# 64-row matmuls on separate row halves of the array for the fifth pass of gate and up

## Chip, cores and metric

One core of one Trainium2 chip. The metric is the device time of one execution in microseconds (us), the median of several runs. Profiles are of one execution, taken by the hardware profiler.

## What is computed

A small vision tower on 16 images of 96 x 96: patches with shifted copies are normalised and projected to 192 features, a class token is put in front (37 positions per image, 592 tokens), one attention layer with 12 heads follows, then a feed-forward layer of experts. The change lies in the last:

```python
probs = softmax(x @ router_w)                    # 8 experts, the best two are kept
g = silu(einsum('bsd,edh->bseh', x, w_gate));  u = einsum('bsd,edh->bseh', x, w_up)
routed = sum_e dense_g[e] * ((g * u) @ w_down[e])               # 8 experts of 192
shared = silu(x @ ws_gate) * (x @ ws_up) @ ws_down              # 768 hidden
alpha = sigmoid(x @ sg_w + sg_b)
h = h + alpha * shared + (1 - alpha) * routed
```

## The kernel before, in words

Everything is transposed for TensorE: features on partitions, tokens in columns (592, padded to 640, two halves of 296 columns). Products are made with near single precision from float16 operands: each operand is split into a high and a low part, and three products (high x high, low weights x high tokens, high weights x low tokens) are added up in PSUM. The 192 features are 128 + 64, so:
- `XAh`, `XAl`: high and low part of token features 0 to 127; `Ah`, `Al` the same of the weights.
- `XB`: the high part of features 128 to 191, twice, in rows 0 to 63 and 64 to 127. `Bw`: the high part of those weights in rows 0 to 63, their low part in rows 64 to 127. One matmul of 128 rows makes two of the products.
- `YC`: the low part of features 128 to 191 in rows 0 to 63, zeros in rows 64 to 127. It lies in the storage of the tile `wring`, and the profile shows it by that name. The memset at L936 clears rows 64 to 127 once the ring's weights have been used.

So each product over the features takes five passes: Ah x XAh, Al x XAh, Bw x XB, Ah x XAl, Bw x YC. In the fifth, half of the array's rows multiply by zeros.

Feed-forward stage on TensorE: the hidden units are 18 blocks `f` of 128 (6 shared, 12 of experts). `gu(i)` with i = 2f + half makes gate (m = 0) and up (m = 1) of one block and one half of the tokens, ten matmuls of 296 columns into two PSUM banks (L580). It waits until product i - 2 has been made (`v_hf`). `down(f)` (L608) has 15 matmuls of 192 columns. The order is gu(2f), gu(2f+1), down(f-2). Between gu's first and second five matmuls of i = 0 stands `router()` (L556, L558): for each of five token tiles the five passes with 9 columns (`YC` and `WC` with 97 rows) and a sixth for the bias. `gates(k)` (L590) transposes the gates in the middle of steps 6 and 7.

Behind each gu(i): ScalarE makes silu of the gate (L817); for experts GpSimd (L863) or, where a block belongs to two experts, VectorE (L1258, two instructions of 64 rows) multiplies by the gate values; VectorE multiplies by up (L1269, `product`); ScalarE rounds to float16 (L824, `ah`), GpSimd takes the rest (L872, `al`). Between these, by fixed places in the code, VectorE does the steps of choosing experts (L1209 to L1245), and ScalarE and VectorE prepare the weights of the next pieces (L719, L972, `ffn_high` and `ffn_low`). After step 15 VectorE adds the shared part into `acc` (L1292). Tokens' high parts come from ScalarE (L736, L737), low parts from VectorE (L1061, `low_parts`).

Of the kernel before, what the change touches and what calls it, by code (L numbers as in the profile page):

```python
# [24 lines left out]
P = 128  # L25
IMAGES, POSITIONS, D = 16, 37, 192
N = IMAGES * POSITIONS
HALF = N // 2
# [17 lines left out]
QC, KC, VC, OC, RC = 0, 384, 768, 960, 1152  # L46
AW = RC + 9
CROWS = 97
# [7 lines left out]
SX, SW, SPIX, SPW, SK, SQ, SP_, SV, SCTX, SH = 64.0, 64.0, 16.0, 256.0, 16.0, 4.0, 256.0, 16.0, 16.0, 16.0  # L56
# [4 lines left out]
FRONT = 3 * P  # L61
# [20 lines left out]
def vit_kernel(nc, x_inner, x_ring, w_inner, w_ring, gb, consts, j_rev, ind, tok_b, cls, tab,  # L82
               aw_a, aw_b, aw_c, f_a, f_b, f_d, gate_rows, out):
    with ExitStack() as ctx:
        def sb(name, shape, dt=F32):
            return ctx.enter_context(nc.sbuf_tensor(name, shape, dt))

        def sem(name):
            return ctx.enter_context(nc.semaphore(name))

        PS = ctx.enter_context(nc.psum_tensor("PS", [P, 8, 512], F32))
# [48 lines left out]
        XAh, XAl, XB = (sb(n, [P, NPAD], F16) for n in ("XAh", "XAl", "XB"))  # L140
        XC = sb("XC", [CROWS, NPAD], F16)
        YC = wring[:, :, :].rearrange("p r d -> p (r d)")[:, 0:NPAD // 2].bitcast(F16)
# [3 lines left out]
        WAh, WAl, WB = (sb(n, [P, AW], F16) for n in ("WAh", "WAl", "WB"))  # L146
        WC = sb("WC", [CROWS, AW], F16)
# [25 lines left out]
        def stages(p):  # L173
            r = (stage, stage, xhl)[p]
            ab = r[:, 0:4 * PC].rearrange("p (k g c) -> p k g c", k=2, g=2)
            return ab[:, 0], ab[:, 1], r[:, 4 * PC:4 * PC + PT_ * D].rearrange("p (f d) -> p f d", f=PT_)

        def split(p):
            r = (piece0, slab, xsq)[p]
            up = r[:, 0:3 * PC].bitcast(F16).rearrange("p (k g c) -> p k g c", k=3, g=2)  # L180
            dn = r[:, 3 * PC:3 * PC + PT_ * D].bitcast(F16).rearrange("p (k f d) -> p k f d", k=2, f=PT_)
            return up[:, 0], up[:, 1], up[:, 2], dn[:, 0], dn[:, 1]
# [25 lines left out]
                   a_first a_xh a_xsq a_s0 a_ring a_bw a_sqr a_cs a_aw a_wh a_sqrt a_hi a_kh a_q1 a_vh a_exp a_pth a_chi a_e a_dup a_sig a_gt  # L208
                   a_fw a_silu a_ah
                   v_one v_ind v_pad v_aw0 v_jm v_jr v_xl v_fold v_wl v_awl v_mk v_stat v_h v_hn v_lo  v_kk v_q2 v_vm v_xr v_sg v_max v_sub  # L210
                   v_rows v_cn v_rd v_lg v_gate v_gx v_fw v_hf v_acc v_fin v_al v_bn
                   g_one g_sg g_al""".split()
        S = {n: sem(n) for n in names}

# [4 lines left out]

            return [XAh[:, cols], XAh[:, cols], XB[:, cols], XAl[:, cols], XC[:, cols]]  # L220

        def yparts(cols, rows=P):

            return [XAh[:, cols], XAh[:, cols], XB[:, cols], XAl[:, cols], YC[0:rows, cols]]

        def wparts(c0, c1):

            return [WAh[:, c0:c1], WAl[:, c0:c1], WB[:, c0:c1], WAh[:, c0:c1], WC[:, c0:c1]]

        def pair_cols(C, p, rows):  # L230

# [62 lines left out]
        def _(pe):  # L294
            mm = nc.tensor.matmul
# [61 lines left out]
            for t in range(TILES):  # L357
                last = mm(PS[:, 1, t:t + 1], sqrows[:, t * P:(t + 1) * P], one[:, :], start=(t == 0), stop=True,
                          skip_group_check=True)
# [4 lines left out]
            for t in range(TILES):  # L364
                tok = slice(t * P, (t + 1) * P)
                mm(PS[:, (6, 6, 7, 7, 2)[t], D * (t % 2):D * (t % 2) + D], inds[:, tok], biasrow[:, :],
                   start=(t % 2 == 0), stop=True, skip_group_check=True).then_inc(S["p_bias"], 1)
# [23 lines left out]
            def tokens_ready(n, half, k):  # L391

                if k in (0, 2):
                    pe.wait_ge(S["a_hi"], 4 * n + 2 * half + (1 if k == 0 else 2))
                if k in (3, 4):
                    pe.wait_ge(S["v_lo"], 4 * n + 2 * half + (1 if k == 3 else 2))
# [4 lines left out]
            for f in range(12):  # L401
                q, g, half = kq_product(f)
                if f == 3:
                    transposes(0, (1, 2, 0), (3, 4))
                c0 = (QC if q else KC) + g * P
                if f >= 4:
                    q4, g4, half4 = kq_product(f - 4)
                    pe.wait_ge(S["v_q2" if q4 else "v_kk"], GROUPS * half4 + g4 + 1)
                cols = slice(half * HALF, (half + 1) * HALF)
                for i, (w, x) in enumerate(zip(wparts(c0, c0 + P), xparts(cols))):  # L410
                    if f in (0, 6):
                        tokens_ready(0, half, i)
                    last = mm(PS[:, 3 + f % 4, 0:HALF], w, x, start=(i == 0), stop=(i == 4))  # L413
                last.then_inc(S["p_q" if q else "p_k"], 1)
# [132 lines left out]

            def router():

                pe.wait_ge(S["v_rows"], 1)  # L550
                pe.wait_ge(S["a_hi"], 8)
                pe.wait_ge(S["v_lo"], 8)
                for t in range(TILES):
                    tok = slice(t * P, (t + 1) * P)
                    for k, (x, w) in enumerate(zip(yparts(tok, CROWS), wparts(RC, RC + 9))):
                        mm(PS[:, 7, 9 * t:9 * t + 9], x, w, start=(t == 0 and k == 0), stop=False,  # L556
                           skip_group_check=True)
                    last = mm(PS[:, 7, 9 * t:9 * t + 9], XO[:, :], WC[:, RC:RC + 9], start=False, stop=True,  # L558
                              skip_group_check=True)
                last.then_inc(S["p_r"], 1)  # L560

            def gu(i):

                f, half = divmod(i, 2)
                if i % (2 * PT_) == 0:
                    pe.wait_ge(S["a_fw"], 6 * (f // PT_) + 6)
                    pe.wait_ge(S["v_fw"], 6 * (f // PT_) + 6)
                if i >= 2:
                    pe.wait_ge(S["v_hf"], i - 1)
                cols = slice(half * HALF, (half + 1) * HALF)  # L570
                Ah, Al, Bw, _, _ = split(f // PT_)
                fc = slice(f % PT_ * P, (f % PT_ + 1) * P)
                for m in range(2):
                    if i == 0 and m == 1:
                        router()
                    w5 = (Ah[:, m, fc], Al[:, m, fc], Bw[:, m, fc], Ah[:, m, fc], Bw[:, m, fc])
                    for k, (w, x) in enumerate(zip(w5, yparts(cols))):
                        if i < 2 and m == 0:
                            tokens_ready(1, i, k)
                        last = mm(PS[:, 3 + 2 * (i % 2) + m, 0:HALF], w, x, start=(k == 0), stop=(k == 4))  # L580
                last.then_inc(S["p_gu"], 1)

            def gates(k):
# [30 lines left out]
            for f in range(FT + 2):  # L614
                for half in range(2):
                    if f < FT:
                        gu(2 * f + half)
                    if 0 <= 2 * f + half - GATE_STEP < 2:
                        gates(2 * f + half - GATE_STEP)
                if f >= 2:  # L620
                    down(f - 2)
# [261 lines left out]
        def _(dve):  # L883
            V = nc.vector
# [48 lines left out]

            dve.wait_ge(S["v_wl"], 4)
            dve.wait_ge(S["p_bw"], 1)
            V.memset(YC[64:P, :], 0.0).then_inc(S["v_rows"], 1)  # L936
            V.memset(CA[:, N:NPAD], 0.0)
            V.memset(CC[:, N:NPAD], 0.0)

# [25 lines left out]
            def ffn_low(p, q):  # L965

                Ah, Al, Bw, Dh, Dl = split(p)
                k, m = divmod(q, 2)
                W, hi, st, r0 = (Al, Bw, Dl)[k], (Ah, Bw, Dh)[k], stages(p)[k], (0, 64, 0)[k]
                part = slice(3 * m, 3 * m + 3) if k == 2 else slice(m, m + 1)  # L970
                dve.wait_ge(S["a_fw"], 6 * p + q + 1)
                V.scalar_tensor_tensor(out=W[r0:P, part], in0=st[r0:P, part], scalar=SW, in1=hi[r0:P, part],  # L972
                                       op0=ALU.mult, op1=ALU.subtract).then_inc(S["v_fw"], 1)

            for k in range(3):
# [76 lines left out]
                                    ALU.subtract, ALU.mult).then_inc(S["v_hn"], 1)  # L1052

            def low_parts(n, banks, part):
                a, b = ((PS[:, banks[0], 0:FRONT], PS[0:64, banks[1], 0:FRONT]) if part == 0 else
                        (PS[:, banks[2], 0:2 * P], PS[0:64, banks[2], 2 * P:4 * P]))
                cols = slice(0, FRONT) if part == 0 else slice(FRONT, NPAD)
                for k, (dst, src, hi) in enumerate(((XAl[:, cols], a, XAh[:, cols]),
                                                     ((XC, YC)[n][0:64, cols], b, XB[0:64, cols]))):
                    dve.wait_ge(S["a_hi"], 4 * n + (k + 1 if part == 0 else 4))  # L1060
                    V.scalar_tensor_tensor(out=dst, in0=src, scalar=SX, in1=hi, op0=ALU.mult,  # L1061
                                           op1=ALU.subtract).then_inc(S["v_lo"], 1)
# [209 lines left out]
            for i in range(2 * FT):  # L1272
# [15 lines left out]
                if i == 2 * ST + 3:  # L1288

                    dve.wait_ge(S["p_dn"], ST)  # L1290
                    for t in range(TILES):
                        V.scalar_tensor_tensor(out=acc[:, t, :], in0=PS[:, t // 2, D * (t % 2):D * (t % 2) + D],  # L1292
                                               scalar=small[:, 38, t:t + 1], in1=h2[:, t, :], op0=ALU.mult,
# [5 lines left out]
            for t in range(TILES):  # L1299
                dve.wait_ge(S["p_end"], t // 2 + 1)  # L1300
                V.scalar_tensor_tensor(out=fin[:, t, 0:D], in0=PS[:, t // 2, D * (t % 2):D * (t % 2) + D],
                                       scalar=1.0 / (SH * SW), in1=acc[:, t, :], op0=ALU.mult,
# [112 lines left out]
```

## Time and profile before

| | |
|---|---|
| median of 3 runs | 173.03 us (172.47 to 173.92) |
| the profiled execution | 173.96 us, its span 172.2 us |
| TensorE busy | 147.6 us, 86% of the span, 1714 matmuls |
| VectorE busy | 121.1 us, 70% |
| ScalarE busy | 90.7 us, 53% |
| GpSimd busy | 41.3 us, 24% |

The span is the time from the first to the last instruction of the program in the profile; the execution's own time has about 1.8 us more around it. PE is TensorE's matmuls, PEld its weight loads, DVE VectorE, ACT ScalarE, POOL GpSimd. A matmul's start is recorded, its end is modelled; matmuls overlap, so a row's time is more than its share of the engine, and the distance between starts tells the rate. Times of rows are us from the start of the span.

### The profile page before, as it was taken

How to read it: one execution, taken by the hardware profiler on the slowest of the kernel's cores; microseconds unless marked ns; L12 is line 12 of the kernel's file. 1: busy time of each engine (PE TensorE's matmuls, PEld its weight loads, DVE VectorE, ACT ScalarE, POOL GpSimd, SP SyncE). 2: the span in 40 equal slices, each digit the busy share in tenths (PEclk: the TensorE clock that was granted, in tenths of full speed). 3: DMA queues.
4: the chain of work that ended last, by engine and by line, in shares of the span. 5: the costliest groups of instructions: out<-in, count | busy, mean ns of one | idle time of the engine just before them, and what ended most of it. 6: DMA issues, size and time to landing. Idle time of an engine off the chain costs nothing.

```text
span 172.2 us, 4275 instructions
## 1 busy us (share of the span) xinstructions
PE 147.6 (86%) x1714; PEld 114.3 (66%) x1714; DVE 121.1 (70%) x297; ACT 90.7 (53%) x198; POOL 41.3 (24%) x55
## 2 busy tenths in 40 slices
PE   0439999949799988939999689999899999999992
PEld 0218777923467977838964468788777778888782
DVE  6299953999899997992378299976695663542753
ACT  0588879630577725533237768756645434343340
POOL 0000010000000000000000035336947858578430
PEclk9999999999999999995699999999999999999999
DMA  5999999000000000007990000048300000000003
GB/s 148 380 368 373 337 229 353 7 0 0 0 0 4 4 4 4 4 0 213 386 371 41 4 0 0 4 117 319 134 4 0 0 0 4 4 0 4 0 0 106
DMA packets 7391, 16.89 MB, mean 98 GB/s; under 512 B 800, under 2 KB 3612, under 8 KB 7372
## 3 DMA queue, kind: packets, MB, share of 16 engines
q1 hardware_dynamic: 7012, 16.29, 27.8%
q10 hardware_dynamic: 360, 0.34, 0.7%
q8 instruction: 13, 0.21, 0.5%
q14 instruction: 6, 0.05, 0.1%
HBM read 16.15 MB, written 0.47 MB: 97 GB/s over the span
## 4 chain that ended last, share of the span: by engine, by line
PE 53%; DVE 28%; ACT 6%; issue 4%; DMA 4%; POOL 2%; SPq 0%; DVEq 0%; POOLq 0%
PE PS L580 20%; PE PS L608 11%; DMA xs<-in_x_inner_dram 4%; PE PS L413 3%; DVE xsq L1128 3%; DVE mx L1124 2%; PE PS L322 2%; DVE piece L972 2%; PE PS L475 2%; PE PS L425 2%; DVE hn L1051 2%; PE PS L343 2%; PE PS L345 2%; PE PS L346 2%; PE PS L309 2%
## 5 line engine op out<-in xcount | busy, mean ns | idle before, releaser
L872 POOL TENSOR_TENSOR kq<-vhl,kq 128x296 f16<-128x296 f32 x35 | 28.7, 820 | 95.1 <-ACT kq L824 95.1
L1269 DVE SCALAR_TENSOR_TENSOR vhl<-PS,vhl 128x296 f32<-128x296 f32 x36 | 16.7, 465 | 21.0 <-POOL vhl L863 12.1
L817 ACT ACTIVATE vhl<-PS 128x296 f32<-128x296 f32 x36 | 14.9, 416 | 26.2 <-PE PS L580 26.2
L824 ACT ACTIVATE kq<-vhl 128x296 f16<-128x296 f32 x36 | 16.1, 446 | 5.7 <-DVE vhl L1269 5.7
L863 POOL TENSOR_TENSOR vhl<-vhl,xs 128x296 f32<-128x296 f32 x14 | 12.6, 902 | 5.5 <-issue 4.8
L1258 DVE TENSOR_TENSOR vhl<-vhl,xs 64x296 f32<-64x296 f32 (+1 forms) x18 | 10.2, 566 | 2.8 <-ACT vhl L817 2.6
L580 PE MATMUL PS<-XAh,piece 128*128 128x296 f16 x48 | 10.0, 289 | 2.0 <-DVE vhl L1269 1.9
L372 PE MATMUL PS<-WAh 128*128 128x512 f16 x41 | 9.5, 379 | 2.5 <-DVE small L1020 2.2
L580 PE MATMUL PS<-XAh,slab 128*128 128x296 f16 x48 | 10.0, 290 | 0.9 <-DVE vhl L1269 0.9
L343 PE MATMUL PS<-whl,xhl 128*128 128x193 f16 (+1 forms) x40 | 10.5, 262 | 0.0
L345 PE MATMUL PS<-whl,xhl 128*128 128x193 f16 (+1 forms) x40 | 10.5, 262 | 0.0
L923 DVE SCALAR_TENSOR_TENSOR we<-slab,gbs,we 128x192 f32<-128x192 f32 x24 | 8.1, 409 | 3.2 <-ACT we L664 3.2
L346 PE MATMUL PS<-whl,xhl 128*128 128x192 f16 (+1 forms) x40 | 10.4, 259 | 0.0
L309 PE MATMUL PS<-slab,gbs 128*32 128x192 f32 x60 | 4.5, 396 | 6.5 <-DMA slab<-in_w_inner_dram 6.5
L580 PE MATMUL PS<-XAh,xsq 128*128 128x296 f16 x48 | 10.0, 290 | 0.0
L372 PEld LDWEIGHTS PS<-WAh 128*128 128x128 f16 x41 | 3.7, 97 | 7.8 <-issue 2.5
L608 PE MATMUL PS<-slab,kq 128*128 128x192 f16 x90 | 8.4, 246 | 0.3 <-DVE t L1292 0.3
L608 PE MATMUL PS<-piece,kq 128*128 128x192 f16 x90 | 8.4, 246 | 0.0
L608 PE MATMUL PS<-xsq,kq 128*128 128x192 f16 x90 | 8.2, 246 | 0.1
L608 PEld LDWEIGHTS PS<-slab,kq 128*128 128x128 f16 x90 | 7.5, 98 | 0.8 <-issue 0.6
L322 PE MATMUL PS<-xsq,one 128*32 128x296 f32 (+1 forms) x32 | 5.7, 483 | 2.8 <-ACT xsq L632 2.8
L608 PEld LDWEIGHTS PS<-xsq,kq 128*128 128x128 f16 x90 | 7.5, 98 | 0.5 <-issue 0.3
(217 smaller groups left out, 409.5 us busy)
## 6 DMA issues: line engine op xcount, KB each, us to landing
slab<-in_w_inner_dram SPq DMA_DIRECT2D x3, 960.0 KB, 9.8
xs<-gate_rows_dram SPq DMA_DIRECT2D x8, 296.0 KB, 6.1
xs<-in_x_inner_dram SPq DMA_DIRECT2D x3, 592.0 KB, 10.8
stage<-in_f_a_dram SPq DMA_DIRECT2D x2, 768.0 KB, 10.6
stage<-in_f_b_dram SPq DMA_DIRECT2D x2, 768.0 KB, 12.1
stage<-in_f_d_dram SPq DMA_DIRECT2D x2, 576.0 KB, 13.1
xhl<-in_f_a_dram SPq DMA_DIRECT2D x1, 768.0 KB, 6.3
xhl<-in_f_b_dram SPq DMA_DIRECT2D x1, 768.0 KB, 7.4
```

The costliest lines, as they stand in the source:

```text
L343: mm(o, xh[0:K, j, tok], wh[0:K, j, :], start=(j == 0 and t % 2 == 0), stop=False, skip_group_check=True)
L345: mm(o, xl[0:K, j, tok], wh[0:K, j, :], start=False, stop=False, skip_group_check=True)
L346: last = mm(o[:, 0:D], xh[0:K, j, tok], wl[0:K, j, :], start=False, stop=(j == CHUNKS - 1), skip_group_check=True)
L372: mm(PS[:, bank, :], WAh[:, 0:P], WAh[:, 0:512], start=True, stop=True)
L580: last = mm(PS[:, 3 + 2 * (i % 2) + m, 0:HALF], w, x, start=(k == 0), stop=(k == 4))
L608: last = mm(o, a[:, f % ABUF, tok], w[:, f % PT_, :], start=(f in (0, ST) and t % 2 == 0 and k == 0), stop=(f in (ST - 1, FT - 1) and k == ...
L817: A(silu[:, i % 2, :], PS[:, 3 + 2 * (i % 2), 0:HALF], ACT.Silu, scale=1.0 / XW).then_inc(S["a_silu"], 1)
L824: A(ah[:, f % ABUF, half * HALF:(half + 1) * HALF], hf[:, i % 3, :], ACT.Copy).then_inc(S["a_ah"], 1)
L863: G.tensor_tensor(sgate[:, i % 2, :], silu[:, i % 2, :], Gb[:, f_expert(f)[0], cols], ALU.mult).then_inc(S["g_sg"], 1)
L872: G.tensor_tensor(al[:, f % ABUF, cols], hf[:, i % 3, :], ah[:, f % ABUF, cols], ALU.subtract).then_inc(S["g_al"], 1)
L1258: last = V.tensor_tensor(sgate[r0:r1, i % 2, :], silu[r0:r1, i % 2, :], Gb[r0:r1, e, cols], ALU.mult)
L1269: V.scalar_tensor_tensor(out=hf[:, i % 3, :], in0=PS[:, 4 + 2 * (i % 2), 0:HALF], scalar=SH / XW, in1=src[:, i % 2, :], op0=ALU.mult, op1= ...
```

## The change

In gate/up the fifth pass becomes a matmul of 64 rows. `YC` now has the low part of the tokens in both row halves. `Bw` keeps gate's weights as they were (high in rows 0 to 63, low in 64 to 127), but for up the halves are exchanged (low in rows 0 to 63, high in 64 to 127). The fifth pass of gate then uses rows 0 to 63 and that of up rows 64 to 127, and the two are issued one behind the other at the end of the step. The router's fifth pass uses rows 0 to 63 alone. The memset of `YC` and its semaphore go, and the low part of the tokens is made for 128 rows.

```diff
-        def yparts(cols, rows=P):
-            return [XAh[:, cols], XAh[:, cols], XB[:, cols], XAl[:, cols], YC[0:rows, cols]]
-        def wparts(c0, c1):
-            return [WAh[:, c0:c1], WAl[:, c0:c1], WB[:, c0:c1], WAh[:, c0:c1], WC[:, c0:c1]]
+        def halves(m):
+            return (slice(0, 64), slice(64, P))[m]
+        def yparts(cols, m=0):
+            return [XAh[:, cols], XAh[:, cols], XB[:, cols], XAl[:, cols], YC[halves(m), cols]]
+        def wparts(c0, c1, rows=CROWS):
+            return [WAh[:, c0:c1], WAl[:, c0:c1], WB[:, c0:c1], WAh[:, c0:c1], WC[0:rows, c0:c1]]
...
             def router():
-                pe.wait_ge(S["v_rows"], 1)
...
-                    for k, (x, w) in enumerate(zip(yparts(tok, CROWS), wparts(RC, RC + 9))):
+                    for k, (x, w) in enumerate(zip(yparts(tok), wparts(RC, RC + 9, 64))):
...
                 for m in range(2):
                     if i == 0 and m == 1:
                         router()
-                    w5 = (Ah[:, m, fc], Al[:, m, fc], Bw[:, m, fc], Ah[:, m, fc], Bw[:, m, fc])
-                    for k, (w, x) in enumerate(zip(w5, yparts(cols))):
+                    w4 = (Ah[:, m, fc], Al[:, m, fc], Bw[:, m, fc], Ah[:, m, fc])
+                    for k, (w, x) in enumerate(zip(w4, yparts(cols))):
                         if i < 2 and m == 0:
                             tokens_ready(1, i, k)
-                        last = mm(PS[:, 3 + 2 * (i % 2) + m, 0:HALF], w, x, start=(k == 0), stop=(k == 4))
+                        mm(PS[:, 3 + 2 * (i % 2) + m, 0:HALF], w, x, start=(k == 0), stop=False)
+                if i < 2:
+                    tokens_ready(1, i, 4)
+                for m in range(2):
+                    last = mm(PS[:, 3 + 2 * (i % 2) + m, 0:HALF], Bw[halves(m), m, fc], yparts(cols, m)[4],
+                              start=False, stop=True)
                 last.then_inc(S["p_gu"], 1)
...
-            V.memset(YC[64:P, :], 0.0).then_inc(S["v_rows"], 1)
...
-                W, hi, st, r0 = (Al, Bw, Dl)[k], (Ah, Bw, Dh)[k], stages(p)[k], (0, 64, 0)[k]
+                W, hi, st = (Al, Bw, Dl)[k], (Ah, Bw, Dh)[k], stages(p)[k]
+                r = halves(1 - m) if k == 1 else slice(0, P)
...
-                V.scalar_tensor_tensor(out=W[r0:P, part], in0=st[r0:P, part], scalar=SW, in1=hi[r0:P, part],
+                V.scalar_tensor_tensor(out=W[r, part], in0=st[r, part], scalar=SW, in1=hi[r, part],
...
             def low_parts(n, banks, part):
+                r = slice(0, (64, P)[n])
...
-                                                     ((XC, YC)[n][0:64, cols], b, XB[0:64, cols]))):
+                                                     ((XC, YC)[n][r, cols], b, XB[r, cols]))):
```

## Rows read from the trace of the kernel before

**Rows 1.** The page: TensorE's granted clock in 40 slices, in tenths.

```profile
PEclk9999999999999999995699999999999999999999
```

**Rows 2.** Busy time by stretch: stretch, length, PE, PEld, DVE, ACT, POOL, clock, DMA, GB/s.

```profile
93.00:101.10 8.10, 5.49 (x61) 3.46 (x60) 4.53 (x14) 5.76 (x14) 0.75 (x1) 1.00 0.01 2
101.10:119.80 18.70, 18.50 (x167) 15.20 (x168) 16.15 (x32) 12.85 (x31) 8.80 (x10) 1.00 0.26 85
119.80:129.90 10.10, 9.16 (x80) 6.88 (x78) 7.69 (x16) 6.24 (x14) 6.65 (x8) 1.00 0.23 88
129.90:136.60 6.70, 6.42 (x61) 5.36 (x61) 3.56 (x7) 3.00 (x8) 5.42 (x7) 1.00 0.00 0
136.60:165.00 28.40, 28.40 (x258) 23.11 (x259) 14.72 (x29) 11.89 (x30) 17.79 (x24) 1.00 0.01 2
```

**Rows 3.** The chain of waits in order of time: start, length, engine and line, count.

```profile
101.10 4.00 PE PS L580 x30
...
106.34 1.27 PE PS L580 x10
...
121.84 0.85 POOL vhl L863
...
128.49 1.31 DVE t L1292 x4
...
131.33 1.27 PE PS L580 x10
...
145.69 1.24 PE PS L608 x15
146.93 2.52 PE PS L580 x20
...
150.69 2.77 PE PS L580 x20
```

**Rows 4.** The order of time on TensorE, where the array's form changes, and after a wait.

```profile
22.54 0.25 PE L346 MATMUL PS<-whl,xhl 128*128 128x192 f16 x1
...
22.71 0.14 PEld L309 LDWEIGHTS PS<-slab,gbs 128*32 128x32 f32 x6 [0.16 <-issue]
...
24.21 0.67 PE L322 MATMUL PS<-xsq,one 128*32 128x296 f32 x4
24.81 0.34 PE L338 MATMUL PS<-whl,oneh 128*128 128x192 f16 x2
...
58.92 0.39 PE L445 MATMUL PS<-kq 32*37 32x37 f16 x26
59.24 0.29 PE L425 MATMUL PS<-WAh,slab 128*111 128x192 f16 x1
...
62.56 0.58 PE L434 MATMUL PS<-jrep,mk 101*101 101x222 f16 x4 [0.61 <-DVE xsq L1128]
...
63.07 0.14 PEld L445 LDWEIGHTS PS<-kq 32*37 32x37 f16 x10 [0.15 <-issue]
...
101.10 0.42 PE L580 MATMUL PS<-XAh,piece 128*128 128x296 f16 x2 [0.43 <-DVE vhl L1269]
...
107.43 0.60 PE L590 MATMUL PS<-cst,whl 128*8 128x128 f32 x4
```

**Rows 5.** The order of time: the router's first and last matmul.

```profile
95.01 0.17 PE L556 MATMUL PS<-WAh,XAh 128*128 128x9 f16 x1 [0.45 <-DVE wring L1061]
...
95.74 0.17 PE L558 MATMUL PS<-WC,XO 97*128 97x9 f16 x1
```

**Rows 6.** The order of time on VectorE: the memset of YC and the next instruction.

```profile
28.48 0.33 DVE L936 MEMSET wring<- 64x320 uint32 x1 [3.34 <-PE PS L309]
28.88 0.10 DVE L937 MEMSET we<- 128x48 f32 x1
```

**Rows 7.** The order of time on VectorE: low parts with 128 and with 64 rows.

```profile
93.19 0.56 DVE L1061 SCALAR_TENSOR_TENSOR XAl<-PS,XAh 128x384 f16<-128x384 f32 x1 [0.70 <-ACT XAh L736]
...
93.66 0.54 DVE L1061 SCALAR_TENSOR_TENSOR wring<-PS,XB 64x384 f16<-64x384 f32 x1
```

More of the change, by code:

```diff
@@ L210, in vit_kernel @@
                    v_one v_ind v_pad v_aw0 v_jm v_jr v_xl v_fold v_wl v_awl v_mk v_stat v_h v_hn v_lo  v_kk v_q2 v_vm v_xr v_sg v_max v_sub
-                   v_rows v_cn v_rd v_lg v_gate v_gx v_fw v_hf v_acc v_fin v_al v_bn
+                   v_cn v_rd v_lg v_gate v_gx v_fw v_hf v_acc v_fin v_al v_bn
                    g_one g_sg g_al""".split()
@@ L1054, in low_parts @@
             def low_parts(n, banks, part):
-                a, b = ((PS[:, banks[0], 0:FRONT], PS[0:64, banks[1], 0:FRONT]) if part == 0 else
-                        (PS[:, banks[2], 0:2 * P], PS[0:64, banks[2], 2 * P:4 * P]))
+                r = slice(0, (64, P)[n])
+                a, b = ((PS[:, banks[0], 0:FRONT], PS[r, banks[1], 0:FRONT]) if part == 0 else
+                        (PS[:, banks[2], 0:2 * P], PS[r, banks[2], 2 * P:4 * P]))
                 cols = slice(0, FRONT) if part == 0 else slice(FRONT, NPAD)
                 for k, (dst, src, hi) in enumerate(((XAl[:, cols], a, XAh[:, cols]),
-                                                     ((XC, YC)[n][0:64, cols], b, XB[0:64, cols]))):
+                                                     ((XC, YC)[n][r, cols], b, XB[r, cols]))):
                     dve.wait_ge(S["a_hi"], 4 * n + (k + 1 if part == 0 else 4))
```

## The prediction

> **What bounds the kernel now.** I read the page first (busy shares, then the slices), then the chain of waits, then busy time by stretch, then single instructions around the places that the change touches. TensorE is busy 86% of the span, and from slice 21 on at the full granted clock (2.4 GHz) [rows 1]. The feed-forward stage runs from 93 to 168 us. Split by what the chain shows [rows 2, 3], it falls into five parts:
> - 93.0 to 101.1: the router's logits, then VectorE and ScalarE steps. TensorE is busy 5.49 of 8.10 us and waits for the first products.
> - 101.1 to 119.8: TensorE bound (18.50 of 18.70 us). The chain is gate/up and down matmuls, except 107.63 to 109.48, where it runs over ScalarE to the gate transposes.
> - 119.8 to 129.9: not TensorE. The chain goes ScalarE 119.80, GpSimd 120.36 and 121.84, VectorE from 123.46 to 129.79. Between the end of step 12 and the down at 129.94 TensorE has five steps of 1.26 and two downs of 1.24 us to do, 8.8 of 10.2 us [rows 3]: 1.4 us are spare.
> - 129.9 to 136.6: one down and one gate/up on the chain, then ScalarE, GpSimd and VectorE from 132.60 to 136.54.
> - 136.6 to 168: TensorE without a gap.
> So a change of the gate/up matmuls counts in full only for those that stand on the chain. By the chain's rows these are x30, x10, x20, x20, x10 before 119.8, x10 at 131.33, x10 at 136.59 and seven of x20: 25 steps of 10 matmuls out of 36. The other eleven (steps 0 to 2, 7, 13 to 17, 19, 20) are covered.
>
> **Removed and added, per gate/up step.** (A step is one gu(i).) Twenty matmuls of 296 columns take 2.52 us where nothing disturbs them [rows 3], so one takes 0.126 us and a step 1.26 us. After the change a step has 8 full matmuls and 2 with 64 rows. The columns are the same; the gain is only that the two halves can stream at the same time: one 0.126 us is saved.
> Against it stands a change of the array's form before and after the pair. The trace has four kinds of such changes, and all look alike [rows 4]: the weight load that follows starts only 0.07 us before the modelled end of the last matmul (22.54 + 0.25 = 22.79, load at 22.71; 24.21 + 0.67 = 24.88, next at 24.81; 62.56 + 0.58 = 63.14, load at 63.07; 58.92 + 0.39 = 59.31, load at 59.24). Into narrow forms and out of them, it is the same. Within one form the next matmul starts 0.126 us after the one before. A 296-column matmul is shown with 0.29 us (0.289 in the list of its durations), so at a change the next starts after 0.289 - 0.07 = 0.22 us: 0.094 us more. The weight load isn't hidden there either. An unhidden load of 128 columns shows as a matmul of 0.30 instead of 0.29 us (two in 0.42 after the wait at 101.10 [rows 4], 0.41 in the pairs with hidden loads): 0.011 us, and some 0.004 from load to matmul. The 111-column weights behind the scores cost more (0.29 us at 59.24 [rows 4], 0.25 for the next), which I keep as the upper end.
> The pair itself: in the score matmuls, 26 of 32 rows each and of different row groups take 0.39 us from first start to last end; without the 0.18 us of the last one that is 0.21 us for 25, 8 ns each [rows 4], far under what each would need alone. So I take the second half to start 4 to 8 ns behind the first.
> Per step: 2 x (0.094 + 0.011 + 0.002) - 0.126 + 0.006 = 0.094, taken as **+0.095 us**: a loss. The nearest rows bound it between -0.12 (no drain) and +0.22 (drain, and the halves one after the other).
> No row shows a change from 128 to 64 rows with all 128 columns; all four change the columns, two the rows too. By the Trainium skill, "TensorEngine Tiling (Array Packing)", Key Properties, a change of tiling mode drains TensorE while a change of tile alone does not; the rows above agree for their kinds. The same page's Theoretical Speedup promises up to 2x for a contraction of at most 64 rows: by that alone the step would gain 0.12 us. I take the rule on the drain, since the rows follow it.
>
> **On the chain.** 25 x 0.095 = +2.4 us. What gives some of it back:
> - Step 5 starts at 103.67 behind a VectorE product (103.14, 0.47 long), 0.05 us after TensorE was ready: -0.05.
> - The halves end sooner against what follows them. Today the next step's first matmul is already 0.16 us under way when the last one of a step ends and releases ScalarE; with the drain it is 0.07 us. So where the chain leaves TensorE for another engine (after steps 6, 12, 18 and 35) it leaves 0.09 us earlier: -0.37.
> - Three pairs of steps take 2.68, 2.77 and 2.77 instead of 2.52 us, waiting for VectorE's two-expert products. Between the trigger and that wait lie one gate/up and one down: 0.095 more, and the release 0.09 earlier, gives 0.19 us of slack, which covers the waits of at most 0.16: -0.66.
> Covered steps: 13 to 17 cost 5 x 0.095 = 0.48 in the stretch with 1.4 us to spare; 19 and 20 cost 0.19 against a stall of 0.41; step 7 costs 0.095 against the 0.19 us before the second gate transpose. Steps 0 to 2 cost 0.29 where TensorE works 5.49 of 8.10 us [rows 2]. Without this cover the eleven would add 1.05. Sum for gate/up: 2.4 - 0.05 - 0.37 - 0.66 = **+1.3 us**.
>
> **The router.** It stands on the chain (95.01 to 95.92) and has six matmuls per tile, each starting 0.025 us after the last, 0.15 us per tile, shown with 0.167 us each [rows 5]. After the change the fifth has 64 rows and stands between full ones: change in (0.167 - 0.07 = 0.097), change out (0.178 - 0.07 = 0.108), two unhidden loads. Per tile 3 x 0.025 + 0.099 + 0.110 + 0.036 = 0.32 us: +0.17, five times **+0.85 us**. VectorE's logits, the exponentials, the table load of 1.28 us and the first products all wait for it in turn, so nothing hides it. Ends: 0, or 1.2 with the dearer loads.
>
> **The memset.** VectorE's clearing of YC's rows 64 to 127 starts at 28.48 and the next instruction at 28.88 [rows 6]. It stands at the head of a VectorE chain that runs without a gap to 49.3; the patches' last matmul (31.96), the row sums and the weights are ready before VectorE asks. **-0.40 us**. Ends: 0 and -0.40. The wait v_rows goes with it and had long been met.
> **At no cost:** the low part of the tokens is made with 128 rows instead of 64: 384 columns take 0.56 us with 128 rows and 0.54 with 64 [rows 7]. The weights' low part keeps 64 rows, only other ones for up. Waits for v_lo move behind the fourth pass; the router waited for all of them already.
>
> Sum: -0.40 + 0.85 + 1.3 = **+1.75 us**. The profiled execution took 173.96 us (span 172.2), so 175.7; on the median of the runs, 173.03, that is **174.8 us**, 1.0% slower. A measurement of this kernel can tell about 1% from no change, that is 171.3 and 174.8.
>
> **Rivals.**
> 1. *No drain at 64 rows: faster.* All kinds of change in the trace also alter the columns; a mere split of the rows could be free. Then each step on the chain gains 0.12. Steps 3 and 4 gain nothing (VectorE's product), and the six behind the two-expert products lose theirs to a longer stall: 23 x 0.12 - 6 x 0.12 = 2.0, memset 0.40, router 0: 173.03 - 2.4 = **170.6 us**. It decides as soon as a change of form costs under 0.063 us (half of 0.126). For it: the gate transposes, with weights of 8 columns, start at 107.43 while the matmul before is shown up to 107.61 [rows 3, 4]; no drain there. Against: all that leave part of the array free for others, 32 or 37 columns, do drain. Chance 0.16.
> 2. *The halves run one behind the other, with the drain.* Both stream 128 output columns, the score matmuls only 37. Then a step costs 0.095 + 0.12 = 0.215: 25 x 0.215 - 1.1 + 0.85 - 0.40 = +4.75: **177.8 us**. Chance 0.12.
> 3. *Dear loads.* Both loads at a change cost the 0.045 us of the 111-column weights: 0.068 more per step, 25 times, and 0.34 in the router: **176.8 us**. Chance 0.07.
> 4. *Better cover.* The slower TensorE also frees VectorE and GpSimd of each other between 101 and 137, and half of the loss there goes: about **174 us**. Chance 0.07.
> By the Trainium skill, "TensorE: Matmul & The Clock Gate", The mechanism (Part 3), row tiles start about 4 ns apart; it speaks against rival 2 and agrees with the 8 ns per score matmul.
>
> **How the numbers follow.** My forecast has the chance 0.58, with its own range 173.8 to 176.0, about evenly on both sides of 174.8: 0.30 slower, 0.28 within. Rival 1 gives faster 0.13 and within 0.03; rivals 2 and 3 slower 0.19; rival 4 within 0.07. So faster 0.13, within 1% 0.38, slower 0.49. Leaving out under half of rival 1 and most of rival 2, the range is 170.5 to 177.0.
>
> **What would show it.** In the changed profile: the first 64-row matmul about 0.22 us after the eighth full one, its partner under 0.01 us behind it, the next step's first load 0.23 us later; ten matmuls in 1.35 us instead of 1.26 where TensorE bounds; the router 1.6 us instead of 0.76; the 2.77 us pairs gone; VectorE's chain 0.4 us earlier at 30 us. If the first 64-row matmul follows after 0.126 us, rival 1 holds; if its partner follows after 0.12 us, rival 2. I am wrong if the step gets shorter than 1.26 us.

## The result and the profile after

The changed kernel took 176.94 us (median of 4 runs, 175.01 to 178.46) against 173.31 us before: ratio 1.0132, interval 1.0071 to 1.0194. The ratio compares runs in the fast state only, so it isn't the quotient of these medians, which lie 3.6 us apart (the changed kernel's 178.46 us is a slow run). Two more comparisons of the same kernel gave 1.0138 (1.0084 to 1.0192) and 1.0159 (1.0096 to 1.0221). It is slower by 1.3 to 1.6%, 2.3 to 2.8 us; 1.75 us had been forecast.

The rows below are from the profile of the third comparison (e9_after; its execution took 175.25 us, its span is 173.4). First the order of time on TensorE in one step; line 583 has the eight full matmuls, line 587 the two of 64 rows. The rows name the form in which the array is used, 128*128 or 64*128 here; where it differs from one matmul to the next, the text speaks of a change of form.

```profile
109.31 0.29 PE L583 MATMUL PS<-XAl,piece 128*128 128x296 f16 x1
...
109.52 0.10 PEld L587 LDWEIGHTS PS<-wring,piece 64*128 64x128 f16 x2 [0.24 <-issue]
109.53 0.30 PE L587 MATMUL PS<-wring,piece 64*128 64x296 f16 x2
```

The first 64-row matmul starts 0.22 us after the last full one. The two together are shown with 0.30 us, no longer than one of them: they start 0.003 us apart. The weights' load starts at 109.52, and 109.31 + 0.29 - 109.52 is 0.08: the reading of [rows 4], at a change of the rows alone. Next the router, whose rows before were [rows 5]:

```profile
94.06 0.17 PE L559 MATMUL PS<-WAh,XAh 128*128 128x9 f16 x1 [0.92 <-DVE wring L1070]
...
94.13 0.17 PE L559 MATMUL PS<-WAh,XAl 128*128 128x9 f16 x1
94.23 0.18 PE L559 MATMUL PS<-WC,wring 64*128 64x9 f16 x1
94.34 0.18 PE L561 MATMUL PS<-WC,XO 97*128 97x9 f16 x1
94.38 0.17 PE L559 MATMUL PS<-WAh,XAh 128*128 128x9 f16 x1
...
95.67 0.41 PE L583 MATMUL PS<-XAh,piece 128*128 128x296 f16 x2
```

A tile takes 94.38 - 94.06 = 0.32 us instead of 0.15, the whole router 1.61 us instead of 0.75. The chain of waits of the same profile:

```profile
120.60 0.42 ACT vhl L825
...
129.28 1.31 DVE t L1301 x4
130.72 1.40 PE PS L616 x15
...
154.48 1.34 PE PS L616 x15
155.82 1.01 PE PS L583 x8
157.06 1.11 PE PS L583 x8
158.41 1.34 PE PS L616 x15
```

From one down to the next a block takes 158.41 - 154.48 = 3.93 us, where it took 3.76 (the undisturbed 2.52 and 1.24 of [rows 3]): two steps of 1.34 and a down of 1.25, the latter with one load that isn't hidden. The stretch that GpSimd and VectorE bound lasts from 120.60 to 130.72, 10.12 us, against 10.14 before (119.80 to 129.94): its five steps cost nothing. The head of VectorE's chain, in the order of time of the kernel before and then of e9_after:

```profile
27.75 0.52 PE L309 MATMUL PS<-wring,gbs 96*32 96x192 f32 x4
...
45.06 0.29 PE L413 MATMUL PS<-XAh,WAh 128*128 128x296 f16 x1 [0.67 <-ACT XAh L736]
```

```profile
27.15 0.52 PE L313 MATMUL PS<-wring,gbs 96*32 96x192 f32 x4
...
27.82 0.10 DVE L944 MEMSET we<- 128x48 f32 x1 [2.36 <-PE PS L313]
...
44.10 0.29 PE L417 MATMUL PS<-XAh,WAh 128*128 128x296 f16 x1 [0.67 <-ACT XAh L744]
```

From the start of the ring's last four matmuls to the first key matmul it is 16.95 us instead of 17.31. The attention stage from there to the first gate/up matmul takes 48.24 us in both.

The stretch from the router's end to the last six matmuls of the last down has these ends in the kernel before, the second of them from its chain:

```profile
95.76 0.41 PE L580 MATMUL PS<-XAh,piece 128*128 128x296 f16 x2
...
167.56 0.67 PE PS L608 x6
```

It took 71.80 us there and takes 73.18 in e9_after (95.67 to 168.85). So the two executions differ by: -0.36 (memset), +0.86 (router), +1.38 in this stretch, and -0.60 because the ring's matmuls start earlier in this one (27.15 instead of 27.75). The sum is +1.28; the spans are 172.2 and 173.4 us. What of the 1.38 is the changes of form, and what is the clock, the experiments tell.

### The profile page after: what moved, and what is told of

Same layout as the page of the kernel before. It is cut to its first block, busy times and chain, and to the rows that moved or that the text cites. A ratio compares the mean times of both kernels' runs of the same rounds, so it can differ in the third digit from the quotient of the medians.

```text
span 176.7 us, 4274 instructions
## 1 busy us (share of the span) xinstructions
PE 155.3 (88%) x1714; PEld 113.5 (64%) x1714; DVE 120.5 (68%) x296; ACT 91.2 (52%) x198; POOL 43.0 (24%) x55
## 4 chain that ended last, share of the span: by engine, by line
PE 57%; DVE 25%; ACT 6%; issue 5%; ACTq 3%; POOL 2%; DVEq 0%; POOLq 0%
PE PS L583 17%; PE PS L616 11%; PE PS L417 5%; PE PS L587 4%; DVE xsq L1137 2%; DVE mx L1133 2%; PE PS L326 2%; DVE piece L980 2%; PE PS L479 2%; PE PS L429 2%; PE PS L313 2%; PE PS L349 2%; PE PS L347 2%; PE PS L350 1%; DVE hn L1059 1%
## 5 line engine op out<-in xcount | busy, mean ns | idle before, releaser
L880 POOL TENSOR_TENSOR kq<-vhl,kq 128x296 f16<-128x296 f32 x35 | 30.5, 871 | 97.8 <-ACT kq L832 97.7
L583 PE MATMUL PS<-XAh,piece 128*128 128x296 f16 x48 | 10.8, 310 | 1.8 <-DVE vhl L1278 1.7
L349 PE MATMUL PS<-whl,xhl 128*128 128x193 f16 (+1 forms) x40 | 10.1, 254 | 0.0
L347 PE MATMUL PS<-whl,xhl 128*128 128x193 f16 (+1 forms) x40 | 10.1, 253 | 0.0
```

The lines of the kernel that those rows point to most:

```text
L347: mm(o, xh[0:K, j, tok], wh[0:K, j, :], start=(j == 0 and t % 2 == 0), stop=False, skip_group_check=True)
L349: mm(o, xl[0:K, j, tok], wh[0:K, j, :], start=False, stop=False, skip_group_check=True)
L880: G.tensor_tensor(al[:, f % ABUF, cols], hf[:, i % 3, :], ah[:, f % ABUF, cols], ALU.subtract).then_inc(S["g_al"], 1)
```

## Experiments

**The changed kernel again (e1_after).**

> The changed kernel once more, with more rounds. Theory: it is 1.3% slower than before (ratio 1.010 to 1.016), of which the change of the array's form makes 1.75 us; in undisturbed gate/up steps ten matmuls take 1.335 to 1.345 us as in its first profile. In that profile TensorE also ran at the half clock from 103.2 to 106.6 us, inside the feed-forward stage, and longer in the attention stage; the kernel before did so only from 77.5 to 84.4 us. Rival: the half clock is part of the change's cost (the longer router makes a longer quiet stretch before step 3); then this profile shows it again at about 97 to 107 us and the ratio stays above 1.010. If the half clock comes by chance, it lies elsewhere or is gone here, and the ratio is nearer 1.010.

Measured: 176.99 us, ratio 1.0138 (1.0084 to 1.0192). Its profile has the half clock (a granted clock of 0.50, that is 1.2 instead of 2.4 GHz) in the feed-forward stage again, from 95.6 to 102.4 us. The page's rows of the granted clock, of the first profile of the changed kernel and of this one:

```profile
PEclk9999999999699999755799969999999999999999
```

```profile
PEclk9999999999999999995799589999999999999998
```

The kernel before has one dip, in slices 19 and 20 [rows 1]. Both of these have another behind it, in slice 24 and in slices 23 and 24, inside the feed-forward stage; the first has longer ones ahead of it too. From the router's end to the first down e1_after takes 10.40 us (96.80 to 107.20), the next kernel, at the full clock there, 9.38: the half clock cost 1.0 us in this execution.

**The router's fifth pass full again (e2_router_full).** Everything else as changed:

```diff
-  enumerate(zip(yparts(tok), wparts(RC, RC + 9, 64)))
+  enumerate(zip(xparts(tok)[0:4] + [YC[0:CROWS, tok]], wparts(RC, RC + 9)))
```

> The changed kernel with the router's fifth pass of 97 rows instead of 64 (rows 64 to 96 of the router's weights are zero), everything else as changed. Theory: the router's ten changes of form cost 0.85 us on the chain; the router takes 0.76 us again instead of 1.6, and the kernel is 0.85 us faster than e1_after (0.6 to 1.1). Rival (the router is covered by ScalarE's table load): no difference to e1_after, within 0.2 us.

Measured: 174.25 us, ratio to before 0.9998 (0.9954 to 1.0043), 2.7 us below e1_after, where 0.6 to 1.1 had been expected. The router takes 0.75 us in its profile, 0.86 less. The medians overstate the rest: the means of the two kernels' runs are 2.0 us apart, and e1_after's had 13.1 us at the half clock against 9.1 here, which by the line given under e9_after is another 0.9. This profile has no half clock between 86 and 174 us, so it is the cleanest look at gate/up alone. From the router's end to the last down it takes 72.82 us (96.08 to 168.90) against 71.80 before: **+1.02 us**. Its rows:

```profile
96.08 0.41 PE L583 MATMUL PS<-XAh,piece 128*128 128x296 f16 x2
```

```profile
107.88 0.25 PE PS L587 x2
108.15 0.42 ACT vhl L825
...
110.00 0.27 PE PS L598
...
130.77 1.40 PE PS L616 x15
...
168.90 0.67 PE PS L616 x6
```

Part by part, before and then here: router's end to the first down 9.18 and 9.38; to the down at 120.86 and 121.88, 15.92 and 16.42; to the one at 129.94 and 130.77, 9.08 and 8.89; to 137.86 and 138.75, 7.92 and 7.98; to the one behind step 35, 26.96 and 27.49; to the last, 2.74 and 2.66. The loss stands in the stretches that TensorE bounds. This also settles the 1.38 us of e9_after: from the first down on (105.41 and 105.46) both profiles take 63.44 us, and up to it e9_after takes 9.74 us against 9.38, with the half clock from 96.9 to 100.4 us. So 1.02 are the changes of form and 0.36 the clock.

By the rows this kernel should be 0.66 us slower than before (1.02 less 0.36 for the memset). The ratio's upper end, 1.0043, is 0.75 us: the runs allow the 0.66, but taken alone they would as well allow none. The size of the cost rests on the profiles and on e5_apart, e6_same_half and e7_pooled.

**The memset on GpSimd, in the kernel before (e3_memset_pool).** The first line goes from VectorE's program, the others come into GpSimd's, which is idle then (and waits for the memset before its next one):

```diff
-            V.memset(YC[64:P, :], 0.0).then_inc(S["v_rows"], 1)
+            pool.wait_ge(S["v_wl"], 4)
+            pool.wait_ge(S["p_bw"], 1)
+            G.memset(YC[64:P, :], 0.0).then_inc(S["v_rows"], 1)
```

> The kernel before with YC's memset moved from VectorE to GpSimd, which is idle then; gate/up and router as before. Theory: VectorE's chain from 28.5 to 49.3 us starts 0.40 us earlier and the kernel is 0.40 us faster than before, ratio 0.998. Rival (something else is late in that chain): 0.

Measured: 173.69 us, ratio 0.9947 (0.9898 to 0.9996). In its profile the way from the ring's last four matmuls to the first key matmul is 16.94 us against 17.31: -0.37.

```profile
27.36 0.52 PE L309 MATMUL PS<-wring,gbs 96*32 96x192 f32 x4
...
44.30 0.29 PE L413 MATMUL PS<-XAh,WAh 128*128 128x296 f16 x1 [0.67 <-ACT XAh L736]
```

The ratio says 0.1 to 1.8 us; the 0.37 are in it, and the runs can't tell more.

**Only the router's fifth pass of 64 rows, in the kernel before (e4_router64).** The same edit of the router as in the change, with the five full passes of gate/up kept.

> The kernel before with only the router's fifth pass cut to 64 rows; gate/up and the memset as before. Theory: ten changes of form in the router, 1.6 us instead of 0.76 from its first to its last start, and the kernel 0.85 us slower than before, ratio 1.005. Rival (hidden): 0.

Measured: 175.18 us, ratio 1.0054 (1.0016 to 1.0092), +0.9 us. One tile in its order of time:

```profile
97.10 0.17 PE L556 MATMUL PS<-WAh,XAl 128*128 128x9 f16 x1
97.20 0.18 PE L556 MATMUL PS<-WC,wring 64*128 64x9 f16 x1
97.31 0.18 PE L558 MATMUL PS<-WC,XO 97*128 97x9 f16 x1
97.34 0.17 PE L556 MATMUL PS<-WAh,XAh 128*128 128x9 f16 x1
```

97.10 to 97.34 is 0.24 us where three intervals of 0.025 had stood: in at 0.10, out at 0.11, and 0.04 to the next start (0.039, of which 0.014 are more than the ordinary interval, behind a load that isn't hidden). The router takes 1.62 us. ScalarE's table load doesn't cover it.

**The halves apart (e5_apart).** On e2's base; the indentation is the edit:

```diff
                     for k, (w, x) in enumerate(zip(w4, yparts(cols))):
                         ...
-                for m in range(2):
-                    last = mm(PS[:, 3 + 2 * (i % 2) + m, 0:HALF], Bw[halves(m), m, fc], ...)
+                    last = mm(PS[:, 3 + 2 * (i % 2) + m, 0:HALF], Bw[halves(m), m, fc], ...)
```

> As e2_router_full, but each step's 64-row matmuls stand apart: gate's behind gate's four full ones, up's behind up's. That is four changes of form per step instead of two, and no second half beside the first. Theory (each change costs 0.095 us plus a load that is not hidden, the gain is the overlap of the halves): a step takes 1.67 us instead of 1.34; where TensorE bounds (25 steps) that is +8.2 us, and with the cover of 13 to 17 used up 8 to 11 us more than e2_router_full. Rival (a change of form is nearly free and the 0.08 us come from the 64-row matmuls themselves): a step takes 1.46 us, +3 us.

Measured: 184.3 us, ratio 1.0602 (1.0544 to 1.066), 10.1 us over e2_router_full. One step in the order of time:

```profile
135.17 0.41 PE L583 MATMUL PS<-XAh,slab 128*128 128x296 f16 x2
...
135.54 0.29 PE L583 MATMUL PS<-XAl,slab 128*128 128x296 f16 x1
135.77 0.30 PE L586 MATMUL PS<-wring,slab 64*128 64x296 f16 x1
136.00 0.42 PE L583 MATMUL PS<-XAh,slab 128*128 128x296 f16 x2
...
136.60 0.30 PE L586 MATMUL PS<-wring,slab 64*128 64x296 f16 x1
136.83 0.30 PE L583 MATMUL PS<-XAh,slab 128*128 128x296 f16 x1
```

136.83 - 135.17 = 1.66 us, as the theory had it (1.67); with free changes it would have been 1.26. In every form change the next matmul comes 0.22 to 0.23 us after the one before it.

**Both 64-row matmuls on rows 0 to 63 (e6_same_half).**

```diff
-  Bw[halves(m), m, fc], yparts(cols, m)[4]          r = halves(1 - m) if k == 1 else slice(0, P)
+  Bw[halves(0), m, fc], yparts(cols, 0)[4]          r = halves(1) if k == 1 else slice(0, P)
```

> As e2_router_full, but both 64-row matmuls of a step use rows 0 to 63 (the low part of up's weights lies in rows 64 to 127 as before the change). Same number of changes of form, no overlap of the halves. Theory: the second starts 0.126 us after the first instead of 0.003, a step takes 1.46 us instead of 1.34: +0.12 for 25 to 33 steps, 3 to 4 us more than e2_router_full. Rival (the overlap is only in the recorded starts, and the second half streams after the first anyway): no difference.

Measured: 178.7 us, ratio 1.0263 (1.0201 to 1.0324), 4.4 us over e2_router_full, a little more than the 3 to 4 expected.

```profile
143.09 0.29 PE L583 MATMUL PS<-XAl,slab 128*128 128x296 f16 x1
143.31 0.42 PE L587 MATMUL PS<-wring,slab 64*128 64x296 f16 x2
143.66 0.42 PE L583 MATMUL PS<-XAh,slab 128*128 128x296 f16 x2
```

Two in 0.42 us instead of 0.30, and 0.35 to the next step instead of 0.23: on one row half they do stream one behind the other. So the overlap of the change's pair is real, and worth 0.12 us a step (1.46 instead of 1.34). From the router's end to the last down it takes 76.01 us (96.81 to 172.82), 3.2 more than e2_router_full; that is the expected size. The rest of the 4.4 isn't in this stretch; this profile has a longer half clock in the attention stage.

**The halves of both steps together (e7_pooled).** In blocks 2 and 4 to 17 the four 64-row matmuls stand behind the sixteen full ones:

```diff
+                if not pooled(i):
+                    pair(i)
+                elif i % 2:
+                    pair(i - 1)
+                    pair(i)
```

> As e2_router_full, but in blocks 2 and 4 to 17 the 64-row matmuls of both steps of a block stand together, behind all 16 full ones: two changes of form per block instead of four. Theory: such a block's two steps take 2.47 us instead of 2.68 (before the change: 2.52) where nothing makes them wait; that gives 0.2 us for each of the shared blocks 2, 4 and 5. In the expert blocks the first step's release comes 1.2 us later, and silu, GpSimd's multiplication and the product (about 2.1 us) outlast the down (1.24 us) that is left in between: 0.6 to 0.9 us of waiting per block, 7 us in all over e2_router_full. Rival (the cost is per 64-row matmul, not per change): 2.68 us as before.

Measured: 189.02 us, ratio 1.0856 (1.0792 to 1.092). One shared block, in the order of time:

```profile
112.78 0.41 PE L586 MATMUL PS<-XAh,piece 128*128 128x296 f16 x2
...
113.66 0.29 PE L586 MATMUL PS<-XAl,piece 128*128 128x296 f16 x1
113.89 0.42 PE L602 MATMUL PS<-wring,piece 64*128 64x296 f16 x4
114.24 0.26 PE L631 MATMUL PS<-piece,kq 128*128 128x192 f16 x1
```

The block's first matmul starts at 111.78, so the two steps take 2.46 us: 2.47 by the theory, 2.68 with four changes of form, 2.52 without any. The cost goes by the change of form, not by the 64-row matmul. In the expert blocks the price was forecast too small: 14.8 us over e2_router_full instead of 7. Its chain there:

```profile
133.53 0.25 PE PS L602 x2
...
134.12 0.44 ACT kq L847
134.56 0.57 ACT xsq L742
135.13 0.32 ACT vhl L840
...
135.83 0.82 POOL vhl L886
136.74 0.48 DVE vhl L1293
137.26 1.18 PE PS L586 x8
```

ScalarE's two silus of this block, in the order of time:

```profile
133.80 0.42 ACT L840 ACTIVATE vhl<-PS 128x296 f32<-128x296 f32 x1 [2.38 <-PE PS L602]
...
135.03 0.40 ACT L840 ACTIVATE vhl<-PS 128x296 f32<-128x296 f32 x1
```

The first step behaves as expected: from its silu at 133.80 it is 2.0 us to the first matmul that waits for its product (135.79), and I had put in 2.1. What I had left out is the second step. Both are released at once, and its silu comes 1.2 us later, because ScalarE's program has between the two silus the rounding of the step before them (line 847) and, in this block, that of the next weights (line 742). The next block's second step, which waits for its product, so starts at 137.26, 3.5 us behind the first silu. From the down at 122.93 to the one at 179.87 a block takes 5.2 us in the mean, where it takes 3.93 in e2_router_full.

**Filling the waits (e8_filled), and the change once more (e9_after).** e8 is the changed kernel with

```diff
+                if i in (2, 3):
+                    keep_warm(0, 5 if i == 2 else 2)
                 if i >= 2:
                     pe.wait_ge(S["v_hf"], i - 1)
```

> The changed kernel with idle matmuls (512 columns, results unused) while TensorE waits before step 2 (five) and step 3 (two), where the first profile of the changed kernel had the half clock from 103.2 us and e1_after's from 95.6 us. Nothing on the chain changes if the clock is full. Theory that part of the measured 2.4 us is the half clock in this stretch, beyond the 1.5 us by the changes of form: the ratio to before falls from 1.014 to about 1.009. Rival (it is all in the changes of form, or the half clock comes from before the router): 1.013 again.

> The changed kernel unaltered, for its time and its share at the half clock beside the kernel before's on the same chip. Theory: the changes of form and the memset make +1.5 us (ratio 1.009), and what is measured above it goes with more time at the half clock, by some 0.3 us of time for each us of it. If the change itself brings more half clock (the TensorE waits between the router and step 3 are the same, the router is longer and thinner), this run again shows more of it than before; if the earlier excess was chance, the two are alike and the ratio is near 1.009.

Measured: e8_filled 175.7 us, ratio 1.0119 (1.0074 to 1.0164), between the 1.009 of the theory and the 1.013 of its rival and nearer the rival; e9_after 176.7 us, ratio 1.0159 (1.0096 to 1.0221). The times alone don't part them. The granted clocks say more. The time at the half clock follows from each run's mean clock c as 2 x (1 - c) x span. Over 57 runs of the kernel before it is 9.7 us in the mean (time 174.30 us), over 16 of the changed kernel 12.5 us (176.54 us). 23 of the 57 had at most 6.9 us of it, none of the 16. The filled kernel had 8.2 us in 6 runs (175.9 us), e2_router_full 9.1 and e4_router64 9.2 us in 12 each. Within the 57 runs of before, one us more of half clock goes with 0.24 us more time (a straight line through them). So 2.8 us more of it are 0.7 us, and with 1.5 us of changes of form and memset that is 2.2 us, the difference of the means.

The 0.7 is an estimate, for what the half clock costs depends on where it lies. From the router's end to the first down e2_router_full takes 9.38 us without it; with 3.4 us of it e9_after takes 0.36 more (from 96.9 us on), e8_filled 1.12 (from 94.3) and the first profile of the changed kernel 1.57 (from 103.2), and e1_after with 6.8 us of it 1.02.

Where the half clock lies: all three profiles of the changed kernel have it inside the feed-forward stage (103.2 to 106.6, 95.6 to 102.4, 96.9 to 100.4 us), and three of the five others with the new gate/up steps (e5, e7, e8, from 94 to 96 us on); none of the four profiles with the old steps (before, e3, e4, e10) has it there. In e8 it ended at 97.7, where e1_after's and e5_apart's went on to 102.4 and 101.2; but it was as short, 3.4 us, in e7_pooled and e9_after, which have no filling, so that the filling ended it isn't shown. That the change brings more of it is thus probable, and what in it does so is open. The long router isn't enough (e4_router64 has it, and no half clock behind it), and neither part alone has more than before in the mean: 9.1 us with the new steps, 9.2 with the new router, 9.7 before. When the first loads land differs too (the ring's last matmul starts between 27.0 and 28.6 us in these profiles), and no run parts that from the rest.

**The memset on GpSimd and the filling (e10_pool_filled).** e3_memset_pool with the filling of e8_filled.

> e3_memset_pool (the kernel before, memset on GpSimd) with the idle matmuls of e8_filled before steps 2 and 3. Theory: 0.4 us from the memset, and where the half clock would run on through steps 1 to 5 it ends sooner: ratio 0.994 to 0.998. Rival (the filling delays steps 2 and 3 or changes nothing): as e3_memset_pool or slower.

Measured: 174.1 us, ratio 0.9971 (0.9928 to 1.0014), half clock 7.8 us in the mean. The filling adds nothing that can be told to e3_memset_pool. That one is the only version whose interval, 0.9898 to 0.9996, lies below 1, and only just; 0.37 us of it can be traced to the memset.

## Why the prediction was right, point by point

- *The drain at 64 rows* (rival 1 against the forecast): 0.222 us from the last full matmul to the first half one wherever the clock is full, as from [rows 4]. A split of the rows alone drains like the others. Rival 1 is out, and with it the gain by the smaller contraction. Why the gate transposes, its best row, cost nothing (0.126 us behind the last matmul, with weights of 8 columns) stays open. By the Trainium skill, "TensorEngine Tiling (Array Packing)", Key Properties, a change of mode drains TensorE: the trace agrees, with 0.096 us beyond the ordinary interval at each change to 64 rows.
- *The halves side by side* (against rival 2): 0.003 us apart in the change, 0.136 us in e6_same_half.
- *The dear loads* (rival 3): an unhidden load cost 0.007 to 0.014 us, not 0.045.
- *Per step +0.095 us*: measured 1.340 against 1.258 us for a step, and 0.011 more for a down; per block 0.175, so 0.0875 per step. The terms were near, not exact: the change to 64 rows cost 0.096 us where 0.107 stood, the change back 0.113 (0.103 at the next start and 0.010 at the one after) where 0.107 stood, the pair's distance 0.003 where 0.006 stood. The difference to 0.095, 25 times, is 0.2 us.
- *What is given back*: the stretches that start with a release of ScalarE got shorter by 0.09 us each, as forecast (before and in e2_router_full, from the first matmul behind step 6 to the second gate transpose 2.05 and 1.96 us; from that behind step 18 to step 21, 4.16 and 4.07; from that behind step 35 to the last down 2.74 and 2.66). The waits for the two-expert products are gone: the downs there take 1.25 us, where they had taken 1.30, 1.40 and 1.40. Sum for gate/up +1.02 where +1.3 stood.
- *The cover of steps 13 to 17*: between the downs at 121.88 and 130.77 e2_router_full takes 8.89 us, e6_same_half with 0.12 us more per step 8.80, and e5_apart with 0.33 more per step 9.18, its cover used up. Before it was 9.08.
- *The router*: +0.86 for +0.85; *the memset*: -0.36 and -0.37 for -0.40.
- *Not in the forecast*: a different share of the half clock. I had taken the granted clock of one profile as given. Of the 2.2 us between the means it is about 0.7, and in part it hid the 0.3 us by which gate/up was put too high. Rival 4 (better cover) didn't come.
- *What was luck*: the parts that the forecast names come to -0.36 + 0.86 + 1.02 = +1.5 us. That the measured 2.3 to 2.8 us still lie near the forecast +1.75 owes something to gate/up's 0.3 us too many standing in for part of the clock's 0.7. By the three ratios, on 173.03 us, the kernel takes 175.3 to 175.8 us, inside the 173.8 to 176.0 that the forecast gave its own mechanism; the median of the first comparison, 176.94 us, lies above that and only 0.06 us inside the whole range, whose upper end of 177.0 was set by rivals that did not come.

## What to carry to other kernels

Before cutting matmuls to half the rows so that two run side by side, count the changes of form: each costs 0.10 to 0.11 us here (drain and unhidden load), two of them more than the 0.126 us that one overlapped pass of 296 columns gives back. It pays only if several half-row passes stand together: four between two changes took 2.46 us a block against 2.52 without any, and only if nobody waits for these steps' results meanwhile. A stream of tiny matmuls is the worst place: with 9 columns each, one half-row pass among six doubled the router's time.

## What the hardware showed unexpectedly

- The release of a step's result comes earlier against the next work when a change of form follows. Behind step 6 ScalarE's silu starts 0.20 us after the next matmul before (107.43 and 107.63) and 0.11 us after it in e2_router_full (108.04 and 108.15). So stretches that hang on ScalarE became 0.09 us shorter by a change that slows TensorE; the forecast had it from the rows, and it is easily overlooked.
- Runs of one kernel differ by their time at the half clock, between 4.1 and 17.1 us of it in the kernel before, with medians near 172.6 us at 4.1 and 175.8 us at 13.6. The attention stage alone (first key matmul to first gate/up matmul) takes 46.7 us with 3.4 us of it, 48.3 with 6.8, and 50.6 with 13.6 to 17.1 (profiles e5 and e8; e1, e2 and before; e4, e6 and the first of the changed kernel).
